# Gather stage: SP issues token loads and one small piece when a matmul placed by a count of PE's program signals

## The reference, cut to what matters

```
grouped = x.reshape(b, s // g, g, d)                      # 32 tokens in a group, d = 512
logits = jnp.einsum('bntd,des->bntes', grouped, Wc) + bc  # 128 = 32 experts x 4 sets
perm = (logits + tie == max over the 32 tokens)           # one token of a group for each expert and set
permuted = jnp.einsum('bntd,bntes->bnesd', grouped, perm)          # the gather
inner = jax.nn.relu(jnp.einsum('bnesd,esdf->bnesf', permuted, W1) + b1)
result_permuted = jnp.einsum('bnesf,esdf->bnesd', inner, W2) + b2  # the scatter stage, not touched
result = jnp.einsum('bnesd,bntes->bntd', result_permuted, perm)
```

## Time and profile before

| | us |
|---|---|
| median of 3 runs | 3052.42 (3048.11 to 3056.96) |
| the profiled execution | 3054.72 |
| its span, first to last instruction | 3052.5 |
| SSM stage | 0 to 2106 |
| gather, first to last pick | 2106.0 to 2505 |
| scatter | 2505 to 3052.5 |

### The profile page before, as it was taken

One profiled execution on the slowest core, in us unless ns is written; L12 is line 12 of the kernel. 1 busy time (PEld: TensorE's weight loads), 2 busy tenths in 40 slices (PEclk: granted clock), 3 DMA queues, 4 the chain that ended last, 5 costly groups with the idle time before them and its releaser, 6 DMA issues.

```text
span 3052.5 us, 134103 instructions
## 1 busy us (share of the span) xinstructions
PE 2896.2 (95%) x59304; PEld 2469.9 (81%) x59304; DVE 2056.2 (67%) x2980; ACT 1698.7 (56%) x3678; POOL 1428.8 (47%) x2287
## 2 busy tenths in 40 slices
PE   5999999999999999999999999997878778999999
PEld 4888888888888888888888888885767667888887
DVE  3777777777777777777777777775444447777775
ACT  3666656666665666656666665663333323555555
POOL 1666767667676666767667676662000001000000
PEclk8999999999999999999999999998999999999999
DMA  3222222222222222222222222216344436877765
GB/s 123 76 71 79 77 74 75 73 78 75 79 73 72 79 70 79 74 76 75 73 76 77 79 74 73 75 42 247 111 126 112 113 99 195 232 214 229 225 204 157
DMA packets 365218, 328.93 MB, mean 108 GB/s; under 512 B 56400, under 2 KB 278096, under 8 KB 363744
## 3 DMA queue, kind: packets, MB, share of 16 engines
q1 hardware_dynamic: 364000, 320.15, 35.4%
q10 hardware_dynamic: 640, 0.20, 0.0%
HBM read 206.96 MB, written 113.31 MB: 105 GB/s over the span
## 4 chain that ended last, share of the span: by engine, by line
PE 90%; DVE 4%; issue 3%; DMA 1%; POOL 1%; SPq 0%; ACT 0%; POOLq 0%; DVEq 0%; ACTq 0%
PE a_proj L920 40%; PE a_mix L920 12%; PE s_rt L1590 8%; PE g_pick_ps L1336 5%; PE a_scan L1031 5%; PE s_w_ps L1560 4%; PE s_rt L1603 4%; DVE g_picked L1303 3%; PE a_scan L1008 3%; PE g_acc_ps L1357 3%; PE a_scan L995 2%; PE a_mix L983 2%; PE a_misc L976 1%; PE a_misc L1049 1%; PE a_scan L1063 0%
## 5 line engine op out<-in xcount | busy, mean ns | idle before, releaser
L920 PE MATMUL a_proj<-wdh,xTh 128*128 128x512 f32 x1024 | 423.0, 413 | 9.1 <-DVE wdl L712 9.1
L1526 ACT COPY s_res<-s_rt 128x512 f32<-128x512 f32 x512 | 263.0, 600 | 279.4 <-PE s_rt L1590 279.4
L920 PE MATMUL a_proj<-wdh,xTl 128*128 128x512 f32 x1024 | 402.7, 393 | 2.2 <-issue 2.2
L920 PE MATMUL a_proj<-wdl,xTh 128*128 128x512 f32 x1024 | 403.9, 394 | 0.0
L1539 DVE TENSOR_TENSOR s_resT<-s_w_ps,s_b 128x1024 f32<-128x1024 f32 x252 | 296.8, 1219 | 141.7 <-PE s_w_ps L1560 141.7
L767 DVE COPY_PREDICATED scan_in<-mask,a_scan 64x512 f32<-64x512 uint32 x512 | 379.1, 740 | 16.0
L445 POOL TENSOR_TENSOR dx<-xs,d_row 64x512 f32<-64x512 f32 x256 | 332.0, 1297 | 15.1
L623 ACT ACTIVATE scan_in<-CT,hsel 64x128 f32<-64x128 f32 x1024 | 325.9, 388 | 4.8
L453 POOL TENSOR_TENSOR yv<-yt,dx 128x512 f32<-128x512 f32 x128 | 188.4, 1472 | 292.5 <-DVE yt L807 292.5
L1303 DVE COPY g_picked<-g_pick_ps 128x1024 f32<-128x1024 f32 x128 | 156.7, 1225 | 226.8 <-PE g_pick_ps L1336 226.8
L587 ACT ACTIVATE raw<-a_proj,rs 128x272 f32<-128x272 f32 x128 | 62.4, 488 | 427.7 <-PE a_proj L920 427.7
(11 more groups left out here) (138 smaller groups left out, 7305.1 us busy)
## 6 DMA issues: line engine op xcount, KB each, us to landing
x<-in_x_dram SPq DMA_DIRECT2D x128, 256.0 KB, 2.7
xn_dram<-xn SPq DMA_DIRECT2D x128, 256.0 KB, 2.4
part_dram<-res SPq DMA_DIRECT2D x128, 256.0 KB, 2.5
g_xn<-xn_dram SPq DMA_DIRECT2D x128, 256.0 KB, 3.0
s_w<-in_w_dram SPq DMA_DIRECT2D x128, 256.0 KB, 3.9
s_part<-part_dram SPq DMA_DIRECT2D x128, 256.0 KB, 3.7
out_dram<-s_out SPq DMA_DIRECT2D x128, 256.0 KB, 2.9
xr<-in_xT_dram SPq DMA_DIRECT2D x126, 256.0 KB, 2.8
```

The lines of the kernel that those rows point to most:

```text
L920: last = nc.tensor.matmul(out, lhs[a], rhs[c], start=(k == 0 and n == 0), stop=(k == nk - 1 and n == 2))
L1526: nc.scalar.copy(res[:, n % 4, :, :], rt_bank[:, n % 3, :, :]).then_inc(res_cp, 1)
```

## The change

SP no longer issues after each pick. A table `refills()` counts PE's instructions through the gather, starting from FIRST = 119, in blocks of BUFFER = 256, and marks in each block the instruction QUIET = 150 behind the block's start by that count. The matmul nearest to the mark increments a new semaphore `refilled`. SP waits for it once for each marked turn (96 of the 128 turns have a mark), then issues up to two token loads, as far as 16 turns ahead, and one small piece: a 128 KB store of `inner` if one is due, else a 128 KB quarter of a one-hot matrix, which before came in one load of 512 KB. The eight token loads of steps 2 and 3 are no longer issued in one go. In the last batch `load_first` waits for the pick as before. PE's program gains no instruction: the signal rides on matmuls that are there.

```
--- before.py
+++ after.py
@@ -1140,6 +1140,7 @@
     LAST = NGB * KD
     PIECES = 8
     PQ = NQ // PIECES
+    BUFFER, QUIET, FIRST = 256, 150, 119
     with ExitStack() as ctx:
         pick_bank = ctx.enter_context(nc.psum_tensor("g_pick_ps", [P, GPT, TW, EX], F32))
         acc_bank = ctx.enter_context(nc.psum_tensor("g_acc_ps", [P, 4, QW, GB], F32))
@@ -1169,6 +1170,25 @@
     acc_cp = sem("acc_cp")
     biased = sem("biased")
     inner_out = [sem(f"inner_out{i}") for i in range(2)]
+    refilled = sem("refilled")
+
+    def refills():
+
+        waves, at = [], FIRST - QUIET
+        for e in range(4 * LAST):
+            n, tq = divmod(e, 4)
+            parts = [4 * TW * GPT + 1]
+            if e == 0 or tq == 3 and n % KD == 0 and 0 < n // KD < NGB - 1:
+                parts.append(2 * GT + 1)
+            if n > 0:
+                parts.append(4 * 4 * QW + (tq == 0))
+            size = sum(parts)
+            offset = -at % BUFFER
+            waves.append(offset if offset < size else None)
+            at += size
+        return waves
+
+    quiet = refills()
 
     xn_dram = keep["xn"].rearrange("k p (b t) c -> b k p t c", t=GT)
     perm_dram = keep["permT"].rearrange("e (b t c) -> b e t c", t=GT, c=P)
@@ -1197,8 +1217,9 @@
         tiles = slice(TW * tq, TW * tq + TW)
         sync.dma_start(xn[n % 4][:, tiles, :], xn_dram[n // KD, n % KD][:, tiles, :]).then_inc(xn_in[n % 4][tq], 16)
 
-    def load_perm(sync, b):
-        sync.dma_start(permT[b % 2][:], perm_dram[b]).then_inc(perm_in[b % 2], 16)
+    def load_perm(sync, b, i):
+        tiles = slice(GT // 4 * i, GT // 4 * (i + 1))
+        sync.dma_start(permT[b % 2][:, tiles, :], perm_dram[b][:, tiles, :]).then_inc(perm_in[b % 2], 16)
 
     def load_w1(sync, k):
         sync.dma_start(w1[:, k, :, :], io["w1"][:, k, :, :]).then_inc(w1_in[k], 16)
@@ -1212,8 +1233,9 @@
         for i in range(2):
             sync.wait_ge(att["pm_out"][i], 16 * (NST // 2))
             sync.wait_ge(att["xn_out"][i], 16 * NST)
-        load_perm(sync, 0)
-        load_perm(sync, 1)
+        for b in range(2):
+            for i in range(4):
+                load_perm(sync, b, i)
         for tq in range(4):
             load_xn(sync, 0, tq)
 
@@ -1231,25 +1253,29 @@
 
     def sync_program(sync, scatter):
         sync.wait_ge(att["res_cp"], 2 * NST)
-        for n in range(2, 4):
-            for tq in range(4):
-                load_xn(sync, n, tq)
-        sync.wait_ge(perm_ps, 1)
-        load_perm(sync, 2)
+        turn, loaded, stored, placed = 0, 8, 0, 8
         for e in range(4 * LAST):
             b, w = divmod(e, 4 * KD)
-            sync.wait_ge(pick_ps, e + 1)
-            if e + 16 < 4 * LAST:
-                load_xn(sync, e // 4 + 4, e % 4)
-            if w == 5 and b + 3 < NGB:
-                sync.wait_ge(perm_ps, b + 2)
-                load_perm(sync, b + 3)
-            if b > 0 and 0 <= w - 5 < PIECES:
-                store_inner(sync, b - 1, w - 5)
+            if quiet[e] is not None:
+                turn += 1
+                sync.wait_ge(refilled, turn)
+                wait(sync, pick_ps, e)
+                for _ in range(2):
+                    if loaded < min(e + 16, 4 * LAST):
+                        load_xn(sync, loaded // 4, loaded % 4)
+                        loaded += 1
+                if b > 0 and stored < PIECES * (b if w >= 5 else b - 1):
+                    store_inner(sync, *divmod(stored, PIECES))
+                    stored += 1
+                elif placed < 4 * min(NGB, b + (4 if w >= 5 else 3)):
+                    sync.wait_ge(perm_ps, placed // 4 - 1)
+                    load_perm(sync, *divmod(placed, 4))
+                    placed += 1
             if b == NGB - 1 and w % 4 == 3:
+                sync.wait_ge(pick_ps, e + 1)
                 scatter["load_first"](sync, w // 4)
-        for piece in range(PIECES):
-            store_inner(sync, NGB - 1, piece)
+        for i in range(stored, PIECES * NGB):
+            store_inner(sync, *divmod(i, PIECES))
 
     def negate_b1(pool):
         pool.wait_ge(small_in, 32)
@@ -1310,7 +1336,7 @@
 
     def transpose_picks(pe, b):
 
-        pe.wait_ge(perm_in[b % 2], 16 * (b // 2 + 1))
+        pe.wait_ge(perm_in[b % 2], 64 * (b // 2 + 1))
         if b == 0:
             pe.wait_ge(ident_ready, 1)
         if b >= 2:
@@ -1321,6 +1347,14 @@
         last.then_inc(perm_ps, 1)
 
     def tensor_program(pe, scatter):
+        PICKS = TW * GPT
+
+        def place_of(offset, part):
+
+            if offset is None or (offset < 4 * PICKS) != (part == 0):
+                return None
+            return min(offset // 4, PICKS - 2) if part == 0 else min(offset // 4 - PICKS, 4 * QW - 2)
+
         def pick(n, tq):
 
             b, k = divmod(n, KD)
@@ -1329,12 +1363,15 @@
                 pe.wait_ge(perm_cp, 2 * (b + 1))
             for i in range(2):
                 wait(pe, pick_cp[i], 4 * n + tq)
+            half = place_of(quiet[4 * n + tq], 0)
             for j in range(TW):
                 t = TW * tq + j
                 for r in range(GPT):
                     rows_ = slice(GRP * r, GRP * r + GRP)
                     last = nc.tensor.matmul(pick_bank[:, r, j, :], xn[n % 4][rows_, t, :], perm[b % 2][rows_, t, :],
                                             start=True, stop=True)
+                    if GPT * j + r == half:
+                        last.then_inc(refilled, 1)
             last.then_inc(pick_ps, 1)
 
         def apply_w1(n, j):
@@ -1351,12 +1388,15 @@
                     pe.wait_ge(perm_cp, j + 1)
                 if 0 < b < NGB - 1 and j < 2:
                     pe.wait_ge(perm_cp, 2 * (b + 1) + j + 1)
+            half = place_of(quiet[4 * n + 4 + j], 1) if n + 1 < LAST else None
             for c in range(QW):
                 q = QW * j + c
                 for e in range(4):
                     last = nc.tensor.matmul(acc_bank[ES * e:ES * e + ES, j, c, :], w1[:, k, 4 * q + e, :],
                                             picked[n % 2][:, 4 * q + e, :], start=(k == 0 and c == 0),
                                             stop=(k == KD - 1), skip_group_check=True)
+                    if 4 * c + e == half:
+                        last.then_inc(refilled, 1)
             if k == KD - 1:
                 last.then_inc(acc_ps, 1)
```

## The result

The changed kernel took 3065.86 us (median of 10 runs, 3061.48 to 3074.37), the kernel before in the same comparison 3052.94 (10 runs, 3048.11 to 3061.43). The ratio is 1.0042, with a 95% interval of 1.003 to 1.0053: 9 to 16 us **slower**. The forecast was 3073, with a range of 3036 to 3098.

What follows compares the result with a forecast made beforehand. The prediction took PE, stalled in the gather by late instruction fetches, as the bound: 3054.7 + 18 (middle) + 2 (tail) = 3074.7 us profiled, where a profiled execution ran 2.3 above the median, so 3073, range 3036 to 3098.

Steps and rivals of the forecast that it cites:

- What bounds the gather: Gather's middle: PE stands at edges of 256-instruction blocks until the next is fetched; 83 blocks of 4.075 us.
- The place of the signal: Gather: signal 209 to 229 instructions behind a crossing (PE passing a block edge), first issue 0.4 us ahead of the next.
- The floor of 3.50 us: Gather: a clean block, fetch start 1.15 us behind the crossing plus 2.35 until PE goes on; work needs 3.43.
- X: Gather: time from first issue to the start of a held-back fetch; mean 3.05 us, ends 2.6 and 3.5.
- The recurrence: Gather: successive block lengths D, D' sum to I (crossing to first issue, 3.1) + X + 2.35 = 8.5 us; mean taken 4.29.
- Tail: End of the gather: stores move to signals while `load_first` keeps its place; +2 us on 11 blocks.
- head: Start of the gather: dealing out the burst of eight loads changes nothing.
- Quarters: Gather: 512 KB one-hot loads cut into quarters remove six large obstacles, at most 4 us, within the count of pieces.
- The fetch slips through: Rival, gather: fetch waits only for the transfer in hand; blocks 3.73 or 3.93 us, 3023 (0.12) or 3040 (0.13).
- The loads are not the cause: Rival, gather: the fetch is late by itself, so moving loads does nothing; 3053 us; chance of same 0.17.
- The marks where the code means them: Rival, gather: signals 1.4 us ahead of a crossing lower the mean block 0.1 to 0.2; inside the range, no own chance.
- Much slower: Rival, gather: a whole bundle counts in every block, X = 3.5, long stalls cost clock; 3090 to 3110 us, chance 0.10.

Runs made afterwards that it cites:

- at 130: The changed kernel with marks recounted (count from 178, lone waits included), signal 122 to 132 instructions behind a block edge: 3045.67 us, 0.9973 of the kernel before.
- at 70: The changed kernel with marks recounted (count from 178, lone waits included), signal 63 to 72 instructions behind a block edge: 3044.91 us, 0.9967 of the kernel before.
- 140: The changed kernel with marks recounted, step tokens in three loads, one per signal, signal 133 to 143 instructions behind a block edge: 3047.7 us, 0.9984 of the kernel before.
- 182 to 192: The changed kernel with marks recounted (count from 178, lone waits included), signal that many instructions behind a block edge: 3062.42 us, 1.0025 of the kernel before.
- the halved copies: Both pick copies halved from step 2: on the changed kernel stripped of later loads and quarters, 3040.41 us; on the changed kernel with all traffic, 3064.57 us.

## Why the prediction was right, point by point

**What bounds the gather: right.** Blocks of 256 instructions, PE passing from one to the next with a stall at most edges, and the number of fetches unchanged. In all 83 blocks of the change PE passes the edge 1.19 us or more behind the end of a fetch. That the traffic beside the fetches, and its place, moves the stalls is shown by the run with small transfers and by the two with one load a signal. By the Trainium skill (Runtime: NRT & Kernel Launch, instruction fetch mechanics) the cost of a block edge is mostly hidden; here it is not, with stalls of up to 2.3 us at edges of the change and a block of 3.88 us whose work was seen to need 3.43.

**The place of the signal: right, and it is the cause.** I said 209 to 229 instructions behind the crossing, with the first issue 3.1 us behind it and 0.3 to 1.5 us ahead of the next. The issue came 2.98 us behind in the mean. The block above has it 0.98 ahead of the next; of 83 bundles 50 lie within 0.3 to 1.5, 28 come further ahead and 5 nearer. One load at this place does the same harm (4.29), the same bundle at 130 does far less (3.98).

**The floor of 3.50 us: wrong, the one step that failed.** "So a clean block is 1.15 + 2.35 = 3.50 us, hardly above the 3.43 of the work: there is no slack, and whatever holds a fetch back is paid in full." Without any transfer a block takes 3.89. So of the 4.075 of the kernel before only some 0.19 are traffic and not 0.58, and the best place could give about 83 x 0.19 = 16 us, not the 48 down to the floor. For the forecast this hardly mattered, since the sum went by the mean start of a fetch and not from the floor; for what I expected of the runs at 70, 130 and 140 it did: they came 26 to 41 us above what I had said. The error was to take three fetches that went well for the rule.

**X: right in the mean.** In the change 64 fetches start more than 1.3 us behind their crossing with a bundle issued ahead of it. From the first issue to the start of such a fetch it is 3.01 us in the mean; I had taken 3.05. By what was issued: one load 2.59 (6 cases), two loads 2.92 (5), a load and a quarter 3.02 (9), two loads and a quarter 3.04 (7), a load and a store 3.14 (21), two loads and a store 2.99 (16). I had 1.9 to 2.6 for one load, 2.95 for a load and a piece, and 3.3 for two loads and a piece. So the second load adds nothing beside a piece, and not 0.7: a fetch does wait for a row of transfers, but not for the sum of them. The Trainium skill (DMA: Bandwidth & Descriptors, queues, rings and completion order) has each DMA engine take turns between its queues packet by packet. By that rule the wait would end with one packet, and the trace does not agree: in the block shown the fetch starts 3.4 us behind the first issue, when only packets of queue 1 have started for 2.4 us.

**The recurrence: right mean, wrong behind it.** D + D' = I + X + 2.35 gave 4.25, and 4.25 is what came, after I had gone up to 4.29. But by it a long block is followed by a short one, with a correlation near -1, and in the trace it is -0.16. And at 182 to 192 it gives 4.03, where 4.24 was measured. Two terms missed and cancelled: fetches start 1.72 us behind the crossing and not 1.9, and from a fetch's start to PE going on it is 2.52 in the mean and not 2.35. That 4.25 was met so closely is in part luck. What fits the places from 63 on is a step: a bundle at 63 to 143 costs some 0.1 us a block, one at 182 to 229 costs 0.35 to 0.4, and where within 182 to 229 it stands is of little account. A reading that is only argued is that in the first case the transfers are through before the next fetch falls due. With first issues at 122 to 132 x 13.4 ns = 1.7 us, X of 3.1 ends at 4.8, when a fetch falls due at 3.98 + 1.3 = 5.3. At 182 x 13.4 ns = 2.4 it ends at 5.5, just behind it. Why the plateau is flat is not explained by this.

**The rest.** Tail: I said +2, it was +0.8; head: nothing, +0.7. Quarters: at most -4, and nothing that can be told. Scatter, DVE, waits for tokens: nothing, as said. The sum of the prediction was 3054.7 + 18 + 2 = 3074.7 for a profiled execution, and 3074.37 came, but 4.1 us of that stand ahead of the gather and have nothing to do with the sum: so near a hit is luck. Against the medians, +12.9, the forecast of +20 was 7 us too high: the middle gave 14.2 and not 18 (352.4 us, just under the 354 to 358 that I had named), the tail 0.8 and not 2, and the rest is what the two traces show beyond the medians. The 14.2 are themselves lowered by the clock: at full clock a block is 0.22 us longer than before and not 0.17.

**The rivals.** The fetch slips through: no; no block length near 3.73 or 3.93 came at this place, with one load or with two. The loads are not the cause: they are, for 0.37 us a block of the change and, against what I held, only for 0.19 before; this rival had more in it than I gave it. The marks where the code means them: the intended place of 150 stands between the 4.00 of 140 and the 4.24 of 190; 150 itself was not run. "Much slower" had long stalls that also cost clock: they do, as seen above, but before no less than in the change.

**Still open.** Why a fetch with nothing beside it starts anywhere from 0.5 to 2.2 us behind the crossing and takes 0.88 to 1.47 us, why the places behind 182 cost the same, and why the halved copies helped in blocks 4 to 34 and not in the 50 behind them.

## What to carry to other kernels

When PE stands on "issue" at regular counts of instructions and a packet of the instruction queue lies ahead of each restart, count where the block edges lie, and keep large DMAs out of the stretch in which the next fetch falls due; here the good stretch was from a quarter to a little over half a block behind the edge, and from seven tenths on it was a loss. Check the place in the trace before trusting a table that was meant to set it: this one was off by some 60 to 80 instructions, and with its signals at 130 the same kernel was 0.27% under the one before instead of 0.42% above it. Look at the granted clock before reading a few us out of two traces. And measure a floor without any load before working out what can be won down to it; three good cases of a trace are no floor.

## What the runs showed of the hardware

- PE's supply of program is a bound of its own: with no other DMA, 256 instructions took 3.88 us a block over 50 blocks, and that did not change when the work beside it was made shorter (copies of 1.22 us down to 0.69). Over 31 other blocks 3.68 was reached.
- A fetch of 16 KB took 0.88 to 1.47 us with nothing beside it (1.12 in the mean), and PE passed the next edge 1.46 us behind its end.
- A DMA issue on SP right behind another took 1.17 us in the mean (up to 1.8) when it met a fetch in flight (74 issues of the run at 70) and 0.43 when it met none; the first issue of a bundle took 0.32 either way.
- A fetch that fell due behind queued transfers started 2.2 to 3.7 us behind their first issue, apart from one at 4.5, 3.0 in the mean; beside a 128 KB store a second 256 KB load added nothing (2.99 against 3.14).
- The granted clock fell from 2.4 to 1.2 GHz around the end of some stalls of PE of 1.2 to 2.7 us at block edges, and the 256 instructions of one such block took 5.50 us.
